# Second self-attention: VectorE's side work moved to between a round's third and fourth maximum, one round later

## The chip, the cores and the metric

The kernel runs on one core of a Trainium2 chip. The metric is the time of one execution on the device in microseconds (us). Below, PE is the matrix engine, DVE the vector engine, ACT the scalar engine, POOL the general-purpose engine, and SP the engine that issues most DMAs; SPq is its queue.

## The reference

Two decoder layers, each of self-attention, cross-attention and a feed-forward block, with a layer norm behind each of the six. The input is 2 x 1024 tokens of 256 numbers. The change lies in the fourth of the six, the self-attention of the second layer, with 16 heads of 16 numbers on 2 batches:

```python
def _layernorm(x, axis=-1, eps=1e-05):
    m = jnp.mean(x, axis=axis, keepdims=True)
    v = jnp.var(x, axis=axis, keepdims=True)
    return (x - m) / jnp.sqrt(v + eps)

def _L1_attn_ref(x, W_qkv, b_qkv, W_proj, b_proj):   # 16 heads of 16, x is (2, 1024, 256)
    B, N, C = x.shape
    qkv = (x @ W_qkv + b_qkv).reshape(B, N, 3, NUM_HEADS, HEAD_DIM)
    q, k, v = jnp.transpose(qkv, (2, 0, 3, 1, 4))
    scores = jnp.einsum('bhqd,bhkd->bhqk', q, k) * SCALE
    attn = jax.nn.softmax(scores, axis=-1)
    out = jnp.einsum('bhqk,bhkd->bhqd', attn, v)
    return jnp.transpose(out, (0, 2, 1, 3)).reshape(B, N, C) @ W_proj + b_proj

x = _layernorm(x + _L0_attn_ref(...), axis=-1)
x = _layernorm(x + _L0_xattn_ref(...), axis=-1)
x = _layernorm(x + _L0_ffn_ref(...), axis=-1)
x = _layernorm(x + _L1_attn_ref(x, L1_attn_W_qkv, L1_attn_b_qkv, L1_attn_W_proj, L1_attn_b_proj), axis=-1)
x = _layernorm(x + _L1_xattn_ref(...), axis=-1)
x = _layernorm(x + _L1_ffn_ref(...), axis=-1)
```

## The kernel before

The program is written engine by engine, with semaphores by hand; nothing reorders it. The second self-attention is in `pe_l1a`, `dve_l1a`, `act_l1a`, `pool_l1a` and `sp_l1a`. It goes over 32 heads (16 per batch) in **rounds** `u` = 0 to 136 (`N_R`); four rounds are one head.

The softmax needs each query's maximum before the exponentials. So the scores are made twice. A first pass makes them with the queries on the partitions, for the maxima alone; a second, some rounds later, makes them with the keys on the partitions, the maximum already taken off through an extra row of the queries' tile. In a round stand:

- **N0 to N3**: four matmuls of the first pass (`natural`, 128x512 each), into banks 0 and 1 in turn. DVE takes the maximum of each: **m0 to m3** (line 1507). N2 waits for m0 and N3 for m1, since they write the same banks; N0 and N1 wait for m2 and m3 of the round before.
- **S**: four matmuls of the second pass (`scores`), for the head of eight rounds ago; ACT makes the exponentials from them (line 1420).
- **W**: the exponentials times the values (`weigh`, 16 matmul records per round), into bank 6.

PE's order in a round is N0, S, N1, N2, W, N3, and then **side work**, which the list `side[u]` sets and which every engine reads. All of it on PE goes through bank 7:

- `rows` (`u` a multiple of 4): PE turns a head's maxima from a column to a row (line 1334), ACT copies the row's leading part (line 1434), DVE takes the rest (line 1536, `s_ml`), and SP writes both into the queries' tile by two DMAs (line 1644).
- `proj` (`u` mod 16 in 1, 3, 5, 7): a quarter of the projection of queries and keys for four heads, six matmuls of 128x512 on PE; ACT takes the leading part out, DVE the rest (`low`, line 1479), which this document calls the **eviction**.
- `values`, `project`, `norm`, `turned`: the values of the second batch (rounds 69 to 72), the output projection of the first batch (rounds 89 to 95), its layer norm in small steps (25 steps for four tiles, from a list `slow`, of which `pump(slow, 4)` takes four in a round), and its transposition (rounds 105 to 111; DVE's part is line 1491). The same list `slow` holds, from round 6 on, the scales of later weights (lines 1457 to 1465, twelve groups of four steps).
- `inverse`: DVE's reciprocals of the softmax's denominators (line 1525), 128x128 each, eight for a group of eight heads. They wait for the DMAs of the group's last head (line 1655), which SP issues, eight for a head in turn into `Zs` and `Zd`, in the round in which that head's sums are ready, behind the `rows` DMAs of the same round. POOL multiplies with them (line 1596).

Where DVE's part of the side work stands, before: the evictions and `turned` go into a list `late` and are done between m0 and m1 of the **next** round; everything else is done right behind m3 of the same round, and then come four steps from `slow`. Every fourth round, m3 is followed by one small reduction (line 1513) that closes a head's maxima.

Of the kernel before, what the change touches and what calls it, by code (L numbers as in the profile page):

```python
# [43 lines left out]
def pump(steps, n):  # L44

    for _ in range(n):
        while steps:
            try:
                next(steps[0])
                break  # L50
            except StopIteration:
                steps.pop(0)
# [21 lines left out]
def program(nc, A, out):  # L74
    ctx = ExitStack()
    with ctx:
        s = {n: ctx.enter_context(nc.semaphore(n)) for n in SEMAPHORES}
# [1139 lines left out]
        N_K = 8 * NH  # L1217
# [6 lines left out]

        side = [[] for _ in range(N_R)]
        for u in range(N_R):
            if u % 4 == 0 and 0 <= (u - 4) // 4 < NH:
                side[u].append(("rows", (u - 4) // 4))
            if 69 <= u < 73:
                side[u].append(("values", 2 * (u - 69)))  # L1230
            if u in (89, 91, 93, 95):
                side[u].append(("project", u - 89))
                if u % 4 == 3:
                    side[u].append(("norm", u - 91))
            if u in (105, 107, 109, 111):
                side[u].append(("turned", (u - 105) // 2))
            if 42 <= u < 128 and u % 32 in (10, 11, 12, 13, 14, 15, 16, 18):
                side[u].append(("inverse", (u - 42) // 32, 128 * (10, 11, 12, 13, 14, 15, 16, 18).index(u % 32), 128))
            if u % 16 in (1, 3, 5, 7) and u // 16 + 1 < 8:
                side[u].append(("proj", u // 16 + 1, (u % 16) // 2))  # L1240
        rest = []
# [232 lines left out]
        def dve_l1a(e, own):  # L1474
            def low(g, u, bk):
                qk, cs, cc = u // 2, slice((u % 2) * 512, (u % 2) * 512 + 512), (C_LQ, C_LK)[u // 2] + g % 4
                hi, lo = TQK[g % 2][qk]
                e.wait_ge(s["s_hi"], 4 * g + u + 1)
                return e.scalar_tensor_tensor(lo[:, cs], PS[:, bk, :], cols[:, cc:cc + 1], hi[:, cs].bitcast(F32),
                                              ALU.add, ALU.subtract)  # L1480

            def values(kt, n, bk):
                shape = dict(a=n, h=16)
                return e.tensor_tensor(V1[:, kt:kt + n, :, 0:16],
                                       PS[:, bk, 0:256 * n].rearrange("p (a h n) -> p a h n", **shape),
                                       rows[:, 2, :].rearrange("p (h n) -> p h n", h=16).unsqueeze(1).to_broadcast([128, n, 16, 16]),
                                       ALU.add)

            def turned(i, bk):
                e.wait_ge(s["t_xh"], 16 + i + 1)  # L1490
                e.tensor_tensor(xl[:, :, i * 256:i * 256 + 256], PS[:, bk, :].rearrange("p (k n) -> p k n", k=2),
                                xh[:, :, i * 256:i * 256 + 256].bitcast(F32), ALU.subtract).then_inc(s["t_xl"], 1)

            for u in range(4):
                low(0, u, u % 2).then_inc(s["s_i"], 1)
            e.wait_ge(s["s_z1"], 1)
            for kt in range(8):
                e.wait_ge(s["s_ip"], 5 + kt)
                values(kt, 1, kt % 2).then_inc(s["s_i"], 1)
            slow, late = [], []  # L1500

            def natural(x, half):
                z, (n, i) = 2 * x + half, divmod(x, 8)
                e.wait_ge(s["s_n"], z + 1)
                if i == 0 and half == 0 and n >= 2:
                    e.wait_ge(s["s_red"], n - 1)
                e.tensor_reduce(nm2[:, n % 2, i, half:half + 1], PS[:, half, :], AX.X, ALU.max,  # L1507
                                negate=True).then_inc(s["s_nr"], 1)
                if z % 16 == 15:
                    e.wait_ge(s["s_nr"], z + 1)  # L1510
                    if n >= 2:
                        e.wait_ge(s["s_p7"], i7["rows", n - 2])
                    e.tensor_reduce(s_nm[:, n % 2, :], nm2[:, n % 2, :, :], AX.X, ALU.min).then_inc(s["s_red"], 1)

            def piece(what):
                if what[0] == "norm":
                    tiles = range(what[1], what[1] + 4)
                    slow.append(norm_steps(e, own, tiles, {j: (s["s_b7"], n_b7["project", j - j % 2]) for j in tiles}))
                elif what[0] in ("proj", "turned"):
                    late.append(what)  # L1520
                elif what[0] == "inverse":
                    _, g, c0, n = what
                    for q in range(2):
                        e.wait_ge(s[f"s_zd{q}"], 128 * (4 * g + 4))
                    e.reciprocal(Zd[:, g % 2, c0:c0 + n], Zd[:, g % 2, c0:c0 + n]).then_inc(s["s_b7"], 1)  # L1525
                elif what[0] == "divide":
                    c0 = what[1]
                    z = Zs[1][:, 1, c0:c0 + 256]
                    e.wait_ge(s["s_b7"], n_b7["inverse", 3, c0, 256])
                    e.tensor_tensor(z, z, Zd[:, 1, c0:c0 + 256], ALU.mult).then_inc(s["s_b7"], 1)  # L1530
                else:
                    e.wait_ge(s["s_p7"], i7[what])
                    if what[0] == "rows":
                        h = what[1]
                        e.wait_ge(s["s_mhd"], h + 1)
                        t = e.tensor_tensor(s_ml[:, h % 2, :], PS[0:8, 7, 0:128], s_mh[:, h % 2, :].bitcast(F32), ALU.subtract)
                    elif what[0] == "values":
                        t = values(what[1], 2, 7)
                    else:
                        jj, bk = what[1], bank7[what]  # L1540
                        e.wait_ge(s["s_xb"], jj + 2)
                        t = e.tensor_tensor(X[:, jj:jj + 2, :], PS[:, bk, :].rearrange("p (a n) -> p a n", a=2),
                                            X[:, jj:jj + 2, :], ALU.add)
                    t.then_inc(s["s_b7"], 1)

            for u in range(N_R):
                x = 2 * u
                if u == 6:
                    slow.append(round_steps(e, own, range(12)))
                if x < N_K:  # L1550
                    natural(x, 0)
                for what in late:
                    if what[0] == "turned":
                        turned(what[1], 7)
                    else:
                        low(what[1], what[2], 7).then_inc(s["s_b7"], 1)
                late = []
                if x < N_K:
                    natural(x, 1)
                    natural(x + 1, 0)  # L1560
                    natural(x + 1, 1)
                for what in side[u]:
                    piece(what)
                pump(slow, 4)
            pump(slow, 99)
            for what in rest:
                piece(what)
                pump(slow, 99)
            for i in range(4, 8):
                turned(i, 2 + i % 2)  # L1570

        def pool_l1a(e):
# [4 lines left out]
            for u in range(N_K // 2):  # L1577
# [3 lines left out]
                if u % 16 == 0 and u // 16 + 1 < 8:  # L1581
                    g = u // 16 + 1
# [5 lines left out]
                    e.tensor_copy(s_wh[:, :], s_wr[:, :]).then_inc(s["s_w"], 1)  # L1588
                    e.wait_ge(s["s_w"], 2 * g + 3)
                    e.tensor_tensor(s_wl[:, :], s_wr[:, :], s_wh[:, :].bitcast(F32), ALU.subtract).then_inc(s["s_w"], 1)  # L1590
                if u >= 52 and u % 32 == 20:
                    g = (u - 52) // 32
                    for half in range(2):
                        z = Zs[g // 2][:, g % 2, half * 512:half * 512 + 512]
                        e.wait_ge(s["s_b7"], n_b7["inverse", g, half * 512 + 384, 128])
                        e.tensor_tensor(z, z, Zd[:, g % 2, half * 512:half * 512 + 512], ALU.mult).then_inc(s["s_zm"], 1)
# [559 lines left out]
        @block.vector  # L2156
        def _(e):
            own = Count(s["dve"])
            dve_l0(e, own)
            dve_rest(e, own)  # L2160
            dve_l1a(e, own)
            dve_l1x(e, own)
            dve_l1f(e, own)

        @block.gpsimd
        def _(e):
            pool_l0(e)
            pool_rest(e)
            pool_l1a(e)
            pool_l1x(e)  # L2170
            pool_l1f(e)
# [78 lines left out]
```

## Time and profile before

| | us |
|---|---|
| three runs, median | 2741.18 |
| lowest, highest | 2738.6, 2742.21 |
| the profiled execution, its own time | 2740.36 |
| its span, first to last instruction | 2738.5 |

| engine | busy us | share of the span |
|---|---|---|
| PE (matmul) | 2453.6 | 90% |
| PEld (weight load, beside PE) | 1710.8 | 62% |
| DVE | 1682.8 | 61% |
| ACT | 1248.4 | 46% |
| POOL | 886.4 | 32% |

The times are of separate executions; the rows below are all of the profiled one, counted from the first instruction of its span. The second self-attention takes the stretch from some 1888 to 2480 us. A row of the timeline gives the start, how long a run of equal instructions took, the engine, the line, the operation and its tiles, the number of instructions, and in brackets how long the engine had been idle and who ended that. In the rows the matmuls N0 to N3 read `PS<-s_K,s_Q`, S reads `PS<-s_Q,s_K`, and W reads `PS<-s_P,s_V`.

### The profile page before, as it was taken

What the parts mean: (1) busy time and instruction counts of PE and PEld (TensorE: products, weight loads), DVE (VectorE), ACT (ScalarE), POOL (GpSimd) and SP (SyncE); (2) the same over time, 40 slices, a digit from 0 to 9 for tenths busy, and PEclk for the clock granted to TensorE, in tenths of its full rate; (3) what the DMA queues carried; (4) which work ended last, traced back from release to release, by engine and by line L of the source; (5) the groups of instructions that cost most, each with busy time, mean ns of one, the idle gap of its engine ahead of it and who ended that gap; (6) DMA issues with size and microseconds to landing.
All of it is one profiled execution on the core that took longest, in us unless ns stands there. A gap on an engine that the chain in (4) does not pass through costs nothing.

```text
span 2738.5 us, 35199 instructions
## 1 busy us (share of the span) xinstructions
PE 2453.6 (90%) x13520; PEld 1710.8 (62%) x13520; DVE 1682.8 (61%) x3009; ACT 1248.4 (46%) x1967; POOL 886.4 (32%) x462
## 2 busy tenths in 40 slices
PE   8999998999999799899999999997898988866763
PEld 7555545744554579788889888995555555534521
DVE  5566655386665335876443444356777778756967
ACT  4555554345555144344444444442565555542442
POOL 4767774366777350102220123001400000004423
PEclk9999999999999999999999999998999999987875
DMA  2000001000000030001010010003243333301000
GB/s 75 13 16 20 12 12 43 12 12 24 12 12 8 22 110 1 31 1 32 31 31 1 31 39 9 1 1 87 57 90 74 76 74 69 72 9 30 1 1 31
DMA packets 57431, 88.08 MB, mean 32 GB/s; under 512 B 13992, under 2 KB 37808, under 8 KB 57264
## 3 DMA queue, kind: packets, MB, share of 16 engines
q1 hardware_dynamic: 57120, 85.77, 12.2%
q8 instruction: 107, 1.75, 0.3%
q14 instruction: 60, 0.49, 0.1%
q10 hardware_dynamic: 144, 0.07, 0.0%
HBM read 37.16 MB, written 2.10 MB: 14 GB/s over the span
## 4 chain that ended last, share of the span: by engine, by line
PE 72%; DVE 18%; issue 3%; ACT 3%; POOL 2%; DMA 1%; SPq 1%; ACTq 0%; DVEq 0%; POOLq 0%
PE PS L85 71%; DVE s_nm L1507 3%; DVE m_gl L1096 2%; DVE PS L575 2%; DVE a_QS L553 1%; ACT a_P L518 1%; DVE a_nm L567 1%; DVE X L270 1%; DVE s_Zd L1525 1%; DVE st_s L231 1%; POOL a_sum L675 1%; DVE x_E L1914 1%; POOL f_H L2119 1%; DVE x_rd L1898 1%; ACT a_QS L472 1%
## 5 line engine op out<-in xcount | busy, mean ns | idle before, releaser
L675 POOL TENSOR_TENSOR a_sum<-a_sum,a_P 128x1024 f32<-128x1024 f32 x192 | 456.2, 2376 | 128.6 <-ACT a_P L518 118.2
L1096 DVE TENSOR_TENSOR m_gl<-m_g,m_gh 128x512 fp32r<-128x512 f32 x288 | 258.1, 902 | 386.4 <-ACT m_g L935 386.4
L518 ACT ACTIVATE a_P<-PS 128x512 f32<-128x512 f32 x512 | 290.1, 596 | 354.7 <-PE PS L85 349.9
L932 ACT ACTIVATE m_gh<-PS,cols 128x512 fp32r<-128x512 f32 x288 | 198.3, 689 | 470.1 <-PE PS L85 470.1
L1507 DVE TENSOR_REDUCE s_nm<-PS 128x1 f32<-128x512 f32 x512 | 336.5, 683 | 106.1 <-PE PS L85 103.2
L567 DVE TENSOR_REDUCE a_nm<-PS 128x1 f32<-128x1024 f32 x256 | 300.4, 1216 | 128.0 <-PE PS L85 128.0
L85 PE MATMUL PS<-m_w2h,m_gh 128*128 128x256 f32 x1152 | 325.2, 282 | 18.9 <-DVE m_gl L1096 18.7
L85 PE MATMUL PS<-m_w2l,m_gh 128*128 128x256 f32 x1152 | 323.8, 281 | 0.0
L85 PE MATMUL PS<-m_w2h,m_gl 128*128 128x256 f32 x1152 | 323.6, 281 | 0.0
L1420 ACT ACTIVATE s_P<-PS 128x1024 f32<-128x1024 f32 x256 | 248.1, 1021 | 127.7 <-PE PS L85 127.3
L85 PE MATMUL PS<-s_K,s_Q 128*128 128x512 f32 x512 | 218.1, 464 | 46.7 <-DVE s_nm L1507 43.7
L85 PE MATMUL PS<-a_P,a_V 128*64 128x512 f32 x1024 | 250.8, 612 | 0.0
L85 PEld LDWEIGHTS PS<-m_w2h,m_gh 128*128 128x128 f32 x1152 | 218.2, 189 | 35.2 <-DVE m_gl L1096 23.6
L85 PE MATMUL PS<-xh,m_w1h 128*128 128x512 f32 x576 | 231.0, 401 | 0.0
L85 PE MATMUL PS<-xh,m_w1l 128*128 128x512 f32 x576 | 227.1, 394 | 0.0
L85 PE MATMUL PS<-a_QS,a_KH 128*128 128x512 f32 x512 | 220.1, 430 | 7.7 <-ACT a_P L518 7.7
L85 PE MATMUL PS<-xl,m_w1h 128*128 128x512 f32 x576 | 225.9, 392 | 0.0
L85 PEld LDWEIGHTS PS<-m_w2h,m_gl 128*128 128x128 f32 x1152 | 219.1, 190 | 10.6
L85 PEld LDWEIGHTS PS<-m_w2l,m_gh 128*128 128x128 f32 x1152 | 218.6, 190 | 0.0
L1151 POOL CAST m_w1h<-m_raw 128x2048 fp32r<-128x2048 f32 x9 | 20.5, 2283 | 603.8 <-PE PS L85 594.1
L85 PE MATMUL PS<-a_QM,a_KL 128*128 128x512 f32 x512 | 202.1, 395 | 0.0
L935 ACT ACTIVATE m_g<-PS,cols 128x512 f32<-128x512 f32 x288 | 196.1, 681 | 0.0
(296 smaller groups left out, 4192.6 us busy)
## 6 DMA issues: line engine op xcount, KB each, us to landing
m_raw<-in_m_w SPq DMA_DIRECT2D x16, 1024.0 KB, 5.1
s_Q<-s_T SPq DMA_DIRECT2D x128, 128.0 KB, 2.4
s_K<-s_T SPq DMA_DIRECT2D x128, 128.0 KB, 2.4
a_KH<-a_KH SPq DMA_DIRECT2D x64, 128.0 KB, 2.4
a_wr<-in_w_qk SPq DMA_DIRECT2D x16, 256.0 KB, 2.8
X<-in_x SPq DMA_DIRECT2D x4, 512.0 KB, 6.1
a_P<-in_w_v SPq DMA_DIRECT2D x8, 256.0 KB, 5.8
a_P<-in_w_o SPq DMA_DIRECT2D x2, 1024.0 KB, 6.0
```

The lines of the kernel that those rows point to most:

```text
L85: return e.matmul(o, l, r, start=start, stop=stop, skip_group_check=shared)
L231: e.bn_stats(st_s[:, j, :], X[:, j, :]).then_inc(own.sem, 1)
L270: e.tensor_scalar(X[:, j, :], X[:, j, :], st_a[:, j, 0:1], st_r[:, 0, j:j + 1], ALU.subtract, ALU.mult).then_inc(s["normed"], 1)
L518: e.activation(a_P[:, g % N_P, half * 512:half * 512 + 512], PS[:, 2 + half, :], ACT.Exp).then_inc(s["a_exp"], 1)
L567: e.tensor_reduce(a_nm[:, n % 2, 8 * a + i:8 * a + i + 1], PS[:, bk:bk + 2, :], AX.XY, ALU.max, negate=True).then_inc(s["a_max"], 1)
L575: e.reciprocal(r, r).then_inc(own.sem, 1)
L675: e.tensor_tensor(o[:, :], a_P[:, (g - 1) % N_P, :] if k == 1 else o[:, :], a_P[:, g % N_P, :], ALU.add).then_inc(s["a_add"], 1)
L932: e.activation(m_gh[r][:, :], PS[:, 4 + n % 3, :], func, bias=cols[:, bcol:bcol + 1]).then_inc(s["m_gh"], 1)
L935: e.activation(m_g0[r][:, :], PS[:, 4 + n % 3, :], func, bias=cols[:, bcol:bcol + 1]).then_inc(s["m_g0"], 1)
L1096: e.tensor_tensor(m_gl[r][:, :], m_g0[r][:, :], m_gh[r][:, :].bitcast(F32), ALU.subtract).then_inc(s["m_gl"], 1)
L1420: e.activation(s_P[w % 4][:, :].rearrange("p (a n) -> p a n", a=2), PS[:, bk:bk + 2, :], ACT.Exp, scale=0.25).then_inc(s["s_exp"], 1)
L1507: e.tensor_reduce(nm2[:, n % 2, i, half:half + 1], PS[:, half, :], AX.X, ALU.max, negate=True).then_inc(s["s_nr"], 1)
```

## The change

DVE's order in a round becomes m0, m1, m2, then all side work that the round **before** left (`late`), then four steps from `slow`, then m3. `values` alone stays behind m3 of its own round. The reciprocals are listed one round later (and the last three at other distances), so that the first group's run in rounds 44 to 49, 51 and 53 instead of behind m3 of rounds 42 to 48 and 50, and the next two groups' 32 and 64 rounds later; POOL's two multiplications with them move from round 52 to round 54. In round 72, PE makes the values before it turns the maxima.

```diff
         for u in range(N_R):
+            if 69 <= u < 73:
+                side[u].append(("values", 2 * (u - 69)))
             if u % 4 == 0 and 0 <= (u - 4) // 4 < NH:
                 side[u].append(("rows", (u - 4) // 4))
-            if 69 <= u < 73:
-                side[u].append(("values", 2 * (u - 69)))
...
-            if 42 <= u < 128 and u % 32 in (10, 11, 12, 13, 14, 15, 16, 18):
-                side[u].append(("inverse", (u - 42) // 32, 128 * (10, 11, 12, 13, 14, 15, 16, 18).index(u % 32), 128))
+            if 43 <= u < 128 and u % 32 in (11, 12, 13, 14, 15, 16, 18, 20):
+                side[u].append(("inverse", (u - 42) // 32, 128 * (11, 12, 13, 14, 15, 16, 18, 20).index(u % 32), 128))
...
-                elif what[0] in ("proj", "turned"):
-                    late.append(what)
+                elif what[0] == "turned":
+                    turned(what[1], 7)
+                elif what[0] == "proj":
+                    low(what[1], what[2], 7).then_inc(s["s_b7"], 1)
...
                 if x < N_K:
                     natural(x, 0)
-                for what in late:
-                    if what[0] == "turned":
-                        turned(what[1], 7)
-                    else:
-                        low(what[1], what[2], 7).then_inc(s["s_b7"], 1)
-                late = []
-                if x < N_K:
                     natural(x, 1)
                     natural(x + 1, 0)
+                for what in late:
+                    piece(what)
+                late = [what for what in side[u] if what[0] != "values"]
+                pump(slow, 4)
+                if x < N_K:
                     natural(x + 1, 1)
                 for what in side[u]:
-                    piece(what)
-                pump(slow, 4)
+                    if what[0] == "values":
+                        piece(what)
+            for what in late:
+                piece(what)
             pump(slow, 99)
...
-                if u >= 52 and u % 32 == 20:
-                    g = (u - 52) // 32
+                if u >= 54 and u % 32 == 22:
+                    g = (u - 54) // 32
```

What this does to the order of instructions is seen on DVE. First the place of an eviction (`s_T`) that is followed by a row's rest (`s_ml`), in rounds 36 and 37; maxima are the rows with 128x1, the small reduction that closes a head is the row with 128x8. Before:

```order
L1513 TENSOR_REDUCE s_nm<-s_nm 128x8
L1507 TENSOR_REDUCE s_nm<-PS 128x1
L1479 SCALAR_TENSOR_TENSOR s_T<-PS,cols,s_T 128x512
L1507 TENSOR_REDUCE s_nm<-PS 128x1 x3
L1536 TENSOR_TENSOR s_ml<-PS,s_mh 8x128
L1507 TENSOR_REDUCE s_nm<-PS 128x1 x5
```

And changed:

```order
L1513 TENSOR_REDUCE s_nm<-s_nm 128x8
L1507 TENSOR_REDUCE s_nm<-PS 128x1 x3
L1479 SCALAR_TENSOR_TENSOR s_T<-PS,cols,s_T 128x512
L1507 TENSOR_REDUCE s_nm<-PS 128x1 x4
L1538 TENSOR_TENSOR s_ml<-PS,s_mh 8x128
L1507 TENSOR_REDUCE s_nm<-PS 128x1 x4
```

The eviction went from behind the first maximum of its round to behind the third, and the row's rest from behind the fourth maximum of that round to behind the third of the next.

The second place is DVE at the first reciprocals of a group (`s_Zd`, from round 42 on). Before:

```order
L1536 TENSOR_TENSOR s_ml<-PS,s_mh 8x128
L1507 TENSOR_REDUCE s_nm<-PS 128x1 x8
L1525 RECIPROCAL s_Zd<-s_Zd 128x128
L1507 TENSOR_REDUCE s_nm<-PS 128x1 x4
L1513 TENSOR_REDUCE s_nm<-s_nm 128x8
L1525 RECIPROCAL s_Zd<-s_Zd 128x128
L1507 TENSOR_REDUCE s_nm<-PS 128x1 x4
```

And changed:

```order
L1538 TENSOR_TENSOR s_ml<-PS,s_mh 8x128
L1507 TENSOR_REDUCE s_nm<-PS 128x1 x9
L1513 TENSOR_REDUCE s_nm<-s_nm 128x8
L1507 TENSOR_REDUCE s_nm<-PS 128x1 x3
L1527 RECIPROCAL s_Zd<-s_Zd 128x128
L1507 TENSOR_REDUCE s_nm<-PS 128x1 x4
```

The first reciprocal stood behind the fourth maximum of round 42 and stands now behind the third of round 44, seven maxima later; the row's rest ahead of it is itself later by three.

## Rows read from the trace of the kernel before

**Rows 1.** The chain that ended last, 1888 to 2430 us, shares by line:

```profile
by line: PE PS L85 68.9%; DVE s_nm L1507 14.2%; issue 4.4%; DVE s_Zd L1525 3.1%; SPq L1655 1.8%; DVE s_ml L1536 1.5%; DMA s_Zd<-s_zt 0.7%; DVE f_ws L1457 0.6%; SPq L1644 0.5%; DMA s_K<-s_T 0.5%; DVE X L1542 0.4%; DVE s_T L1479 0.4%; ACT s_P
```

**Rows 2.** Two stretches: us, busy PE, PEld, DVE, ACT, POOL; granted clock; DMA:

```profile
1960.00:2024.00 64.00, 62.63 (x444) 36.99 (x443) 50.01 (x88) 38.77 (x48) 6.33 (x6) 1.00 0.37 83
...
2062.00:2064.00 2.00, 2.00 (x17) 0.60 (x16) 0.70 (x2) 0.00 (x0) 0.00 (x0) 0.50 0.99 215
```

**Rows 3.** Timeline, a round without side work:

```profile
1995.18 0.73 PE L85 MATMUL PS<-s_K,s_Q 128*128 128x512 f32 x2
1995.72 2.67 DVE L1507 TENSOR_REDUCE s_nm<-PS 128x1 f32<-128x512 f32 x4 [0.69 <-PE PS L85]
...
1997.06 0.19 PEld L85 LDWEIGHTS PS<-s_K,s_Q 128*128 128x128 f32 x1 [0.41 <-DVE s_nm L1507]
1997.49 1.07 PE L85 MATMUL PS<-s_P,s_V 128*32 128x256 f32 x16
1999.03 2.67 DVE L1507 TENSOR_REDUCE s_nm<-PS 128x1 f32<-128x512 f32 x4 [0.64 <-PE PS L85]
```

**Rows 4.** Timeline, rounds with a reciprocal: N2, then m3 and the next m3:

```profile
2071.56 0.50 PE L85 MATMUL PS<-s_K,s_Q 128*128 128x512 f32 x1 [0.86 <-DVE s_nm L1507]
...
2073.53 0.69 DVE L1507 TENSOR_REDUCE s_nm<-PS 128x1 f32<-128x512 f32 x1 [0.74 <-PE PS L85]
...
2077.64 0.69 DVE L1507 TENSOR_REDUCE s_nm<-PS 128x1 f32<-128x512 f32 x1 [0.73 <-PE PS L85]
```

**Rows 5.** Timeline, DVE: m3 before and behind a round with a group of weight scales:

```profile
1931.49 0.69 DVE L1507 TENSOR_REDUCE s_nm<-PS 128x1 f32<-128x512 f32 x1 [0.74 <-PE PS L85]
...
1935.50 0.69 DVE L1507 TENSOR_REDUCE s_nm<-PS 128x1 f32<-128x512 f32 x1 [0.74 <-PE PS L85]
```

**Rows 6.** Timeline, a round with an eviction (PE and DVE), up to its m3:

```profile
1988.99 0.39 PE L85 MATMUL PS<-s_K,s_Q 128*128 128x512 f32 x1
...
1989.42 0.69 DVE L1507 TENSOR_REDUCE s_nm<-PS 128x1 f32<-128x512 f32 x1 [0.72 <-PE PS L85]
...
1990.02 0.74 DVE L1479 SCALAR_TENSOR_TENSOR s_T<-PS,cols,s_T 128x512 fp32r<-128x512 f32 x1
...
1990.13 0.61 PE L85 MATMUL PS<-s_K,s_Q 128*128 128x512 f32 x2
...
1990.68 1.28 DVE L1507 TENSOR_REDUCE s_nm<-PS 128x1 f32<-128x512 f32 x2
...
1992.02 0.28 PE L1334 MATMUL PS<-ident,s_nm 128*8 128x128 f32 x1
...
1992.22 0.69 DVE L1507 TENSOR_REDUCE s_nm<-PS 128x1 f32<-128x512 f32 x1 [0.26 <-PE PS L85]
```

**Rows 7.** Timeline, the first reciprocal of a group and the DMAs it waits for:

```profile
2051.71 0.68 SPq L1644 DMA_DIRECT2D s_Q<-s_mh  x1
...
2057.61 0.69 DVE L1507 TENSOR_REDUCE s_nm<-PS 128x1 f32<-128x512 f32 x1 [0.63 <-PE PS L85]
...
2058.03 0.59 SPq L1655 DMA_DIRECT2D s_Zd<-s_zt  x1
...
2059.92 0.95 DVE L1525 RECIPROCAL s_Zd<-s_Zd 128x128 f32<-128x128 f32 x1 [1.61 <-DMA s_Zd<-s_zt]
...
2061.47 0.80 PE L85 MATMUL PS<-s_K,s_Q 128*128 128x512 f32 x1 [2.51 <-DVE s_nm L1507]
...
2062.20 1.94 PE L85 MATMUL PS<-s_P,s_V 128*32 128x256 f32 x16
...
2064.90 0.69 DVE L1507 TENSOR_REDUCE s_nm<-PS 128x1 f32<-128x512 f32 x1 [1.90 <-PE PS L85]
```

**Rows 8.** Timeline, DVE: m3 ahead of the third group's first reciprocal, and the two next:

```profile
2330.82 0.69 DVE L1507 TENSOR_REDUCE s_nm<-PS 128x1 f32<-128x512 f32 x1 [0.33 <-PE PS L85]
...
2338.32 0.69 DVE L1507 TENSOR_REDUCE s_nm<-PS 128x1 f32<-128x512 f32 x1 [1.90 <-PE PS L85]
...
2343.23 0.69 DVE L1507 TENSOR_REDUCE s_nm<-PS 128x1 f32<-128x512 f32 x1 [0.36 <-PE PS L85]
```

## The prediction, made blind

> **What bounds it now.** I went from the page to the chain of waits, then to the busy time by stretch, and from there to the timeline of single rounds. The chain through the second self-attention is two engines taking turns: PE 68.9% on the matmul line, DVE 14.2% on the maxima, 3.1% on the reciprocals and small shares of the row's rest and the weight scales [rows 1]. By busy time PE looks full in the middle of it, 62.63 of 64 us [rows 2]. The timeline says more [rows 3]. In a round without side work, N3 starts at 1995.18 and m3 0.54 later; m3 and m0 to m2 of the next round follow each other without a gap, four in 2.67, so 0.67 each. N2's weight load is released at 1997.06, the moment m0 ends (1995.72 + 2 x 0.67), W starts 0.43 later, and 1.00 behind W the next N3. That is a loop: 0.54 + 0.67 + 0.67 + 0.43 + 1.00 = 3.31 us, and m3 to m3 is 3.31 (1995.72 to 1999.03). What stands on DVE between m3 and m0 lengthens this loop by all that it takes. But ahead of m3 DVE is idle for 0.64, since m2 ends while PE is in W: that gap is where the change puts the work.
>
> **Side work in the gap.** A piece of length d costs d now, and max(0, d - 0.64) in the gap.
>
> 1. Reciprocals. With one behind m3 the round is 4.11 (2073.53 to 2077.64) [rows 4], so d = 4.11 - 3.31 = 0.80; in the gap 0.16 is left. 3 groups of 8: 24 x 0.64 = 15.4 saved. Where a row's rest shares the round the saving is the same 0.64.
> 2. Weight scales. 4.01 from m3 to m3 [rows 5], d = 0.70, of which 0.06 is left. Twelve groups; the three ahead of the first W, and what then overlaps an eviction, I count for nothing: 9 x 0.64 = 5.8.
> 3. Rows' rests. 1992.22 to 1995.72 is 3.50 [rows 3, 6], d = 0.19, wholly covered. Of 32, only seven stand in a round whose gap is otherwise empty and that follows no eviction: 1.3.
> 4. The layer norm's steps, four to a round like the scales and of like length. Six rounds without an eviction, at 0.64, one of them shared with a row: 3.6.
> 5. The wait for the denominators' DMAs. In two of three groups the first reciprocal holds DVE 1.61 us [rows 7] and more: these rounds take 7.29 (2057.61 to 2064.90) and 7.50 [rows 7, 8] where 4.11 is usual, and the one behind the second 4.91 (2338.32 to 2343.23) where 4.3 is (4.11 and the row's 0.19). 3.2 + 3.4 + 0.6 = 7.2. Part of it is the clock: behind 2.51 us of idle PE, N2 takes 0.80 and W 1.94, against 0.50 and 1.07, at a granted 0.50 [rows 2 to 4, 7]. Does the wait come back? SP issues in order. The row's two DMAs wait for its rest, which is now behind m2 of the next round, some 2.0 us (three maxima) later; the last denominator DMA stands 6.32 behind the first of them (2051.71, 2058.03), so it goes out near 2060.0 and, landing 1.9 later as now (2058.03 to 2059.92), is there at 2061.9. The reciprocal has moved by seven maxima: m3 of its old round at 2057.61, one plain round of 3.31, then m3 itself and m0 to m2, 2.67, makes 2063.6. It comes 1.7 behind the data. I take the whole 7.2.
>
> Saved: 15.4 + 5.8 + 1.3 + 3.6 + 7.2 = 33.3.
>
> **What the move costs.**
>
> 6. Evictions. They now stand between m0 and m1, which costs nothing: m1 must wait for N1 anyway. m0 starts 0.43 behind N0's start (1988.99, 1989.42), so m1 could start 0.43 behind N1's 1990.13, at 1990.56, and m2 end 1.28 later, at 1991.84 [rows 6]. The eviction (0.74, of which 0.14 overlaps with its neighbours as m0's start and m1's show: 0.60) would then end at 1992.44, while m3's data are there at 1992.22. With what a start costs (0.02 to 0.04), 0.26 per eviction; it stays in the loop because the next m0 is behind m3. 28 run in the rounds; the first three have no W behind them and DVE works there without a gap either way: 25 x 0.26 = 6.5.
> 7. Bank 7. In 14 rounds PE turns a row straight behind an eviction. It does so at 1992.02 now [rows 6] and must wait until 1992.5, with N0, S and N1 behind it. N2 follows N0 by 1.36 (1988.99 to 1990.35, below) and N0 the turn by some 0.1: 1994.0. m0, behind an m3 that starts at 1992.48, ends at 1993.8, and N2's weights take up to 0.19 from there [rows 3]. So 0 to 0.2 shows; 0.13 taken: 14 x 0.13 = 1.8.
> 8. Collisions. In four rounds an eviction and norm steps, which are both hidden today (one between m0 and m1, the other behind a PE busy with the projection), meet in one gap: the steps' 0.70 finds no room there; I take 0.5 each, between 0 and 0.70, 2.0. DVE's four `turned` pieces move like evictions, 4 x 0.25 = 1.0, and three of them meet a reciprocal whose saving of item 1 is then gone, 3 x 0.64 = 1.9. The four output projections, 0.1 each: 0.4. These are estimates from the rows of the single pieces.
>
> Costs: 6.5 + 1.8 + 2.0 + 2.9 + 0.4 = 13.6. Edits that I put at nothing: POOL's multiplications two rounds later (their results are wanted at round 89 or past the end) and the swap of values and rows in round 72 (bank 7 makes one wait for the other either way).
>
> **Sum.** 33.3 - 13.6 = 19.7 less. The profiled execution took 2740.36 (span 2738.5); 2720.7. It lies 0.8 under the median of the three runs, 2741.18, so against that: 2721.
>
> **Bounds.** The gap shows as 0.64 in a plain round, 0.74 where there is side work [rows 3, 4] and 0.26 in an eviction round [rows 6]. Its pieces have their round to themselves, so 0.64 is the nearest; at 0.74 some 38 whole uses give 3.8 more, and at 0.26 they give 14 less, which I hold for far. An eviction costs between 0 (6.5 better) and its whole 0.74 (25 x 0.48 = 12 worse). Of item 5, at worst the DMA wait proper comes back, 2 x 1.7 = 3.4. Together 8 better to 12 or 13 worse.
>
> **Rivals.**
>
> *Evictions cost their whole length.* If m1 and m2 run late after a projection (or PE, held at bank 7, makes them late), no gap is left in those rounds and all 0.74 lies in the loop: 12 worse, 2733. For it: only 0.26 is idle there [rows 6]. Against it: m2 ends 0.4 ahead of m3's data by the same rows.
>
> *PE is the bound, and nothing moves.* If the matmuls need the 3.31 themselves, DVE's order is free: 2741. For it: PE busy 98% [rows 2]. Against it: from N0 to N2 is 1.36 in the eviction round (1988.99; the pair that starts at 1990.13 takes 0.61 and its second 0.39 of that, so N2 starts at 1990.35) and 1.54 in the plain one (N0 at 1995.18 + 0.73 - 0.39 = 1995.52, N2 at 1997.06), so PE waits 0.18 while it counts as busy; and with a reciprocal it stands 0.86 before N2, released by a maximum [rows 3, 4, 6]. The Trainium skill, "Perfetto Trace Analysis", section "Identifying the Most-Contended Engine", says to take the engine with the highest occupancy and optimise that first, which here is PE, so that by it this reordering of DVE saves nothing. The same section calls matmul occupancy a poor measure; the 0.18 of waiting inside busy time agrees with that.
>
> *The clock falls, slower.* If PE, waiting at bank 7 or at N1 behind a late eviction, were idle long enough for its clock to fall to the lower level, as it did to 1.2 GHz in the DMA wait, each such round would pay what that one did beyond the wait: 7.29 less 3.31, 0.80 and 1.65 (m3's end to the reciprocal's start, 2058.27 to 2059.92) = 1.53. 25 x 1.53 = 38, so 2741 - 20 + 38 = 2759. It decides between 0.86 us of idle, where N2 still takes 0.50, and 2.51, where it takes 0.80 [rows 4, 7]; item 7 makes 0.5.
>
> **How the numbers follow.** Forecast 0.80, costly evictions 0.13, PE the bound 0.04, clock 0.03. Range 2713 to 2734: the forecast with its bounds, and the first rival. 0.2% is 5.5 us, about what a measurement of this kernel can tell: above 2735.7 is no change. The forecast and nearly all of the first rival lie below: faster 0.91, same 0.06, slower 0.03.
>
> **What would show it.** Reciprocal rounds at 3.45 to 3.6 instead of 4.11 to 4.3; scale rounds at 3.35; row rounds that follow no eviction at 3.31; eviction rounds at 4.7 instead of 4.42, counted from m3 to m3; no idle time of DVE before a reciprocal; plain rounds unchanged at 3.31. It is wrong if plain rounds change, if SP's gathers come late, if a reciprocal still waits for its DMA, or if eviction rounds exceed 5.

## The result, and the profile after

| | before | after |
|---|---|---|
| median of the runs, us (4 and 4) | 2739.89 | 2714.89 |
| lowest and highest | 2734.14, 2742.21 | 2713.13, 2717.37 |
| the profiled execution, its own time (span) | 2740.36 (2738.5) | 2717.37 (2715.5) |

The ratio is 0.9912, with a 95% interval of 0.9894 to 0.9931: faster by 0.9%, 25.0 us, where 19.7 were forecast. From m3 of round 0 to m3 of round 127 the changed kernel takes 493.32 us instead of 519.73, 26.41 less in the profiled pair, so the whole gain lies in these rounds. The profiled executions differ by only 23.0: the one of after reaches its first maximum 2.7 later, in stages that the change does not touch, and takes 0.8 more behind the last m3.

The chain that ended last, shares by line, changed kernel, 1888 to 2410 us:

```profile
by line: PE PS L85 64.9%; DVE s_nm L1507 21.8%; DVE s_T L1479 3.6%; issue 2.2%; DVE s_Zd L1527 1.5%; PE PS L1334 0.9%; SPq L1627 0.6%; DMA s_K<-s_T 0.5%; DVE X L1544 0.5%; DVE xl L1491 0.5%; DVE st_s L231 0.4%; SPq L1657 0.4%; DVE s_V L1484
```

Against [rows 1], the reciprocals' share is halved (3.1% to 1.5%). The weight scales and the row's rest (0.6% and 1.5%) no longer stand among the shares shown, nor does the DMA into `s_Zd`. The matmul line fell from 68.9% to 64.9%, and the maxima rose from 14.2% to 21.8%. The evictions came in, with 3.6% instead of 0.4%, and the turn through bank 7 with 0.9%: the price that the prediction expected.

Busy time and clock of 64 us in the middle, in the order of [rows 2]:

```profile
1957.00:2021.00 64.00, 62.67 (x453) 36.83 (x446) 50.15 (x89) 39.10 (x49) 6.34 (x6) 1.00 0.41 92
```

PE counts as busy for 62.67 of 64 us where it was 62.63 [rows 2], at the same granted clock. This view alone shows neither the gain that was to be had nor the one that was made.

Timeline of DVE, changed kernel, the rounds of the first reciprocals:

```profile
2059.38 0.69 DVE L1507 TENSOR_REDUCE s_nm<-PS 128x1 f32<-128x512 f32 x1 [0.63 <-PE PS L85]
...
2062.08 0.94 DVE L1527 RECIPROCAL s_Zd<-s_Zd 128x128 f32<-128x128 f32 x1
2062.94 1.25 DVE L1507 TENSOR_REDUCE s_nm<-PS 128x1 f32<-128x512 f32 x2
...
2065.81 0.93 DVE L1527 RECIPROCAL s_Zd<-s_Zd 128x128 f32<-128x128 f32 x1
2066.67 2.50 DVE L1507 TENSOR_REDUCE s_nm<-PS 128x1 f32<-128x512 f32 x4
2069.08 0.94 DVE L1527 RECIPROCAL s_Zd<-s_Zd 128x128 f32<-128x128 f32 x1
2069.94 2.62 DVE L1507 TENSOR_REDUCE s_nm<-PS 128x1 f32<-128x512 f32 x4
2072.48 0.94 DVE L1527 RECIPROCAL s_Zd<-s_Zd 128x128 f32<-128x128 f32 x1
2073.34 0.63 DVE L1507 TENSOR_REDUCE s_nm<-PS 128x1 f32<-128x512 f32 x1
```

The maximum behind a reciprocal is an m3. From m3 to m3 the rounds take 3.56 (2059.38 to 2062.94), 3.73 with a row's rest in it, 3.27 (2066.67 to 2069.94) and 3.40, against 4.11 [rows 4]. DVE has no idle time left ahead of m3. The first reciprocal waits for nothing; the last DMA for it was issued here:

```profile
2058.43 0.59 SPq L1657 DMA_DIRECT2D s_Zd<-s_zt  x1
```

With the 1.9 that such a DMA took [rows 7] its data are there at 2060.3, 1.75 ahead of the reciprocal at 2062.08. The prediction said 1.7.

Timeline of DVE, changed kernel, two rounds with weight scales:

```profile
1934.15 2.61 DVE L1507 TENSOR_REDUCE s_nm<-PS 128x1 f32<-128x512 f32 x4
1936.68 0.41 DVE L1457 TENSOR_REDUCE f_ws<-f_w 128x1 f32<-128x256 f32 x1
1937.13 0.15 DVE L1461 TENSOR_SCALAR f_ws<-f_ws 128x1 f32<-128x1 f32 x1
1937.31 0.16 DVE L1465 RECIPROCAL f_ws<-f_ws 128x1 f32<-128x1 f32 x1
1937.44 2.68 DVE L1507 TENSOR_REDUCE s_nm<-PS 128x1 f32<-128x512 f32 x4
```

m3 to m3 is 3.29 (1934.15 to 1937.44), where such a round took 4.01 [rows 5].

Timeline of PE and DVE, changed kernel, the eviction round that answers to [rows 6]:

```profile
1985.51 0.69 DVE L1507 TENSOR_REDUCE s_nm<-PS 128x1 f32<-128x512 f32 x1 [0.73 <-PE PS L85]
...
1988.25 1.29 DVE L1507 TENSOR_REDUCE s_nm<-PS 128x1 f32<-128x512 f32 x2 [0.46 <-PE PS L85]
...
1989.45 0.74 DVE L1479 SCALAR_TENSOR_TENSOR s_T<-PS,cols,s_T 128x512 fp32r<-128x512 f32 x1
1990.11 1.38 DVE L1507 TENSOR_REDUCE s_nm<-PS 128x1 f32<-128x512 f32 x2
...
1990.25 0.27 PE L1334 MATMUL PS<-ident,s_nm 128*8 128x128 f32 x1 [0.38 <-DVE s_T L1479]
```

The eviction now stands between m2 (behind m1 at 1988.25) and m3 (1990.11). The round is 4.60 (1985.51 to 1990.11), 0.18 longer than the 4.42 of before. PE waits 0.38 at bank 7 for the eviction. Plain rounds are 3.31 as before.

The stage by the prediction's items, its counts shared out over the rounds, from the starts of m3 in both traces (us; each round's difference, summed):

| rounds | predicted | measured |
|---|---|---|
| weight scales, with what is counted for evictions and bank 7 in these rounds (1 to 17) | -5.3 | -5.46 |
| rows' rests alone (seven rounds) | -1.3 | -1.35 |
| norm steps (93 to 103, odd) | -3.6 | -4.33 |
| the reciprocals' rounds with the DMA wait and the evictions and `turned` among them (43 to 57, 75 to 89, 107 to 117) | -17.1 | -21.27 |
| eviction and norm in one gap (98 to 104, even) | +3.3 | +3.15 |
| output projections (90 to 96, even) | +0.4 | -0.32 |
| other evictions and bank 7 | +3.9 | +3.17 |
| sum | -19.7 | -26.41 |

### The profile page after: what moved, and what is told of

Read it like the earlier page. It is cut to its first block, busy times and chain, and to the rows that moved or that the text cites. A ratio compares the mean times of both kernels' runs of the same rounds, so it can differ in the third digit from the quotient of the medians.

```text
span 2715.5 us, 35197 instructions
## 1 busy us (share of the span) xinstructions
PE 2450.4 (90%) x13518; PEld 1709.8 (63%) x13520; DVE 1686.8 (62%) x3009; ACT 1250.1 (46%) x1967; POOL 886.2 (33%) x462
## 3 DMA queue, kind: packets, MB, share of 16 engines
q8 instruction: 107, 1.75, 0.3%
## 4 chain that ended last, share of the span: by engine, by line
PE 71%; DVE 20%; issue 3%; ACT 3%; POOL 2%; DMA 1%; SPq 0%; ACTq 0%; DVEq 0%; POOLq 0%
PE PS L85 70%; DVE s_nm L1507 4%; DVE m_gl L1096 2%; DVE PS L575 2%; DVE a_QS L553 1%; ACT a_P L518 1%; DVE a_nm L567 1%; DVE X L270 1%; DVE s_T L1479 1%; DVE x_E L1916 1%; DVE x_rd L1900 1%; DVE st_s L231 1%; POOL f_H L2121 1%; POOL a_sum L675 1%; ACT a_QS L472 0%
```

## The experiments

The theory is the prediction's: the loop m3, m0, N2, W, N3, m3 is the bound, side work outside it is free up to the gap's length, and reciprocals listed later don't wait for their DMAs. The rivals are that only idle time seen ahead of m3 is free, that PE is the bound, and that the whole gain is the DMA wait. Every ratio is to the kernel before, of runs on the same chip.

### Only the reciprocals later, still behind m3

From the kernel before; POOL's multiplications move with them:

```diff
-            if 42 <= u < 128 and u % 32 in (10, 11, 12, 13, 14, 15, 16, 18):
+            if 44 <= u < 128 and u % 32 in (12, 13, 14, 15, 16, 17, 18, 20):
```

> The kernel before, with one edit: the reciprocals (and the multiplications behind them) are listed two rounds later, still behind the fourth maximum, and nothing else moves. Loop theory (the change gains by its place: side work behind m0 and ahead of m3 is covered by the loop's slack, and behind m3 it is not): only the wait for the denominators' DMAs goes, some 7 us less than before (ratio 0.997), and rounds with a reciprocal stay at 4.1 to 4.3 us from m3 to m3. Rival (PE is the bound, the whole gain of the change is the DMA wait and the clock that fell with it): all of the change's 25 us, ratio 0.991.

Median 2733.19 (12 runs) against 2739.39 (17); ratio 0.9977 [0.9962, 0.9992]. DVE's timeline:

```profile
2072.67 0.69 DVE L1507 TENSOR_REDUCE s_nm<-PS 128x1 f32<-128x512 f32 x1 [0.74 <-PE PS L85]
2073.28 0.94 DVE L1525 RECIPROCAL s_Zd<-s_Zd 128x128 f32<-128x128 f32 x1
...
2076.79 0.69 DVE L1507 TENSOR_REDUCE s_nm<-PS 128x1 f32<-128x512 f32 x1 [0.74 <-PE PS L85]
```

No reciprocal waits for a DMA any more and the stage is 8.0 shorter (511.77), near the 7.2 of item 5. The rounds still take 4.12 (2072.67 to 2076.79), with 0.74 idle ahead of m3 that nothing uses. The later table alone buys the DMA wait, with the low clock that came with it, and nothing else; the rest is the place in the round.

### The changed order with the reciprocals one round earlier

From the changed kernel, the table of before:

```diff
-            if 43 <= u < 128 and u % 32 in (11, 12, 13, 14, 15, 16, 18, 20):
+            if 42 <= u < 128 and u % 32 in (10, 11, 12, 13, 14, 15, 16, 18):
```

> The changed kernel with the reciprocals listed as in the kernel before, so that they run one round earlier than in the changed kernel, at the same place between m2 and m3. By its trace the first reciprocal of a group comes 1.7 us behind its data; one round is 3.3 us. Loop theory with item 5 of the prediction: the first reciprocal of the first and third group waits for its DMA again, some 1.6 us, and the clock may fall with it: 3 to 7 us more than the changed kernel, ratio to before 0.992 to 0.994. Rival (the DMA wait had gone because of the place, not of the later round): as the changed kernel, ratio 0.991, no idle time before a reciprocal.

Median 2720.61 (6 runs); ratio 0.9935 [0.9920, 0.9950], stage 500.46. DVE's timeline at the first reciprocal:

```profile
2048.77 2.67 DVE L1507 TENSOR_REDUCE s_nm<-PS 128x1 f32<-128x512 f32 x4 [0.64 <-PE PS L85]
2053.01 0.95 DVE L1527 RECIPROCAL s_Zd<-s_Zd 128x128 f32<-128x128 f32 x1 [1.56 <-DMA s_Zd<-s_zt]
2053.88 0.63 DVE L1507 TENSOR_REDUCE s_nm<-PS 128x1 f32<-128x512 f32 x1
```

The wait is back, 1.56 against 1.61 [rows 7], and the round (2048.77 to 2053.88) takes 5.11 where it is 3.31 in the changed kernel. With the rows' rests one round later, SP's DMAs are later too: the last one goes out 2.34 behind the m3 shown first (at 2051.11), where it was 0.42 before (2058.03 behind 2057.61 [rows 7]). The expectation named the first and the third group; the second waits too, 2.27, and the third 1.96. Against the changed kernel the stage is 7.1 longer. So the delay of the table was needed for this order.

### How much fits into the gap

From the changed kernel: reciprocals of ones, whose result nobody reads, in plain rounds between m2 and m3, two rounds of each width up to 128 columns, one of 160; and one behind m3 of round 126:

```diff
+            PAD = {26: 32, 27: 32, 30: 64, 31: 64, 58: 96, 59: 96, 62: 112, 63: 112, 118: 128, 119: 128, 122: 160}
...
                 pump(slow, 4)
+                if u in PAD:
+                    padded(PAD[u])
                 if x < N_K:
                     natural(x + 1, 1)
+                if u == 126:
+                    padded(64)
```

> The changed kernel plus 11 useless reciprocals on a tile of their own, each in a round without any side work, between m2 and m3, in widths of 32 (rounds 26, 27), 64 (30, 31), 96 (58, 59), 112 (62, 63), 128 (118, 119) and 160 (122), and one of 64 behind m3 of round 126. The output is the reference's. From the reciprocals of 128 and 256 (0.94 and 1.75 us, 0.14 overlapped) these are pieces of length 0.19, 0.40, 0.60, 0.70, 0.80 and 1.00. Loop theory: rounds without side work are 3.31; 26 to 63 stay so, 118 and 119 become 3.4, 122 becomes 3.6, and the one behind m3 costs its whole 0.40 (round 127 at 3.7). If the gap were the 0.64 that the prediction read from the idle time, 62 and 63 would be 3.37 and 118, 119 3.47. Rival (PE is the bound in such rounds): all at 3.31 up to 1.0, the one behind m3 too.

One run (2715.5 us); the rounds are read within its trace. DVE's timeline at 112 columns, then behind m3 of round 126 (maxima are line 1514 here):

```profile
2124.37 2.68 DVE L1514 TENSOR_REDUCE s_nm<-PS 128x1 f32<-128x512 f32 x4 [0.33 <-PE PS L85]
2126.97 0.84 DVE L1507 RECIPROCAL s_pad<-ones 128x112 f32<-128x112 f32 x1
2127.73 2.62 DVE L1514 TENSOR_REDUCE s_nm<-PS 128x1 f32<-128x512 f32 x4
2130.27 0.84 DVE L1507 RECIPROCAL s_pad<-ones 128x112 f32<-128x112 f32 x1
2131.03 0.65 DVE L1514 TENSOR_REDUCE s_nm<-PS 128x1 f32<-128x512 f32 x1
...
2384.55 0.69 DVE L1514 TENSOR_REDUCE s_nm<-PS 128x1 f32<-128x512 f32 x1 [0.62 <-PE PS L85]
2385.15 0.54 DVE L1507 RECIPROCAL s_pad<-ones 128x64 f32<-128x64 f32 x1
...
2388.26 0.69 DVE L1514 TENSOR_REDUCE s_nm<-PS 128x1 f32<-128x512 f32 x1 [0.74 <-PE PS L85]
```

Records of 0.34, 0.54 and 0.74 leave the round at 3.30 to 3.31. At 0.84 the first round is 3.36 (2124.37 to 2127.73) and the second 3.30 (to 2131.03); at 0.94 they are 3.28 and 3.39, where the changed kernel without them has 3.22 and 3.31; at 1.145 the round is 3.66, and the next one gives 0.05 back (3.26). Behind m3, a record of 0.54 makes the round 3.71 (2384.55 to 2388.26): 0.40 dearer, all of it but the 0.14 that overlaps. So a piece is free between m2 and m3 up to a record of some 0.84, that is a length of 0.70, and costs its whole length behind m3. PE is not the bound: a wait that DVE puts into the loop shows at once.

### Evictions back between m0 and m1, the rest in the gap

From the changed kernel:

```diff
                     natural(x, 0)
+                for what in late:
+                    if what[0] in ("proj", "turned"):
+                        piece(what)
...
                 for what in late:
-                    piece(what)
+                    if what[0] not in ("proj", "turned"):
+                        piece(what)
```

> The changed kernel, with the evictions and the turned pieces back between m0 and m1, where the kernel before has them; all other side work stays between m2 and m3. Loop theory: eviction rounds go from 4.6 to 4.8 us back to 4.42, and the four rounds in which an eviction meets norm steps from 5.05 to 5.4 back to some 4.5; 10 us less than the changed kernel, 35 less than before (ratio 0.987). Rival (the place does not matter, only that work is a round later, or PE is the bound): as the changed kernel, ratio 0.991.

Median 2702.91 (4 runs); ratio 0.9868 [0.9852, 0.9883], stage 482.62: faster than both kernels. PE and DVE at the eviction round answering to the one above:

```profile
1981.58 0.69 DVE L1507 TENSOR_REDUCE s_nm<-PS 128x1 f32<-128x512 f32 x1 [0.56 <-PE PS L85]
...
1983.81 0.74 DVE L1479 SCALAR_TENSOR_TENSOR s_T<-PS,cols,s_T 128x512 fp32r<-128x512 f32 x1
1984.46 1.28 DVE L1507 TENSOR_REDUCE s_nm<-PS 128x1 f32<-128x512 f32 x2
...
1985.81 0.27 PE L1334 MATMUL PS<-ident,s_nm 128*8 128x128 f32 x1
1986.01 1.29 DVE L1507 TENSOR_REDUCE s_nm<-PS 128x1 f32<-128x512 f32 x2 [0.27 <-PE PS L85]
```

The round is 4.43 (1981.58 to 1986.01), and PE turns the row without waiting. The four collisions fall from 5.42, 5.31, 5.25 and 5.05 to 4.85, 4.77, 4.72 and 4.48, the three rounds in which `turned` meets a reciprocal from 4.50, 4.26 and 4.44 to 4.07, 3.79 and 4.01. These are the costs of items 6 to 8, most of them undone; the four collisions still stand above the 4.62 and three times 4.42 of before.

### Evictions alone between m2 and m3, all else as before

From the kernel before, the loop over `late` moved behind m1 and m2 (behind `natural(x + 1, 0)`).

> The kernel before with one edit: the evictions and the turned pieces stand between m2 and m3 of their round instead of between m0 and m1; all else as before. Loop theory: eviction rounds go from 4.42 to 4.6 to 4.8, without the collisions with norm steps; some 6 to 7 us more than before, ratio 1.0025. Rival (an eviction is hidden by PE's projection wherever it stands): ratio 1.000.

Median 2742.83 (11 runs) against 2738.89 (15); ratio 1.0018 [1.0007, 1.0028], stage 526.83. Eviction rounds take 4.59 to 4.64, and rows' rounds behind one 3.72 instead of 3.50. This is the one part of the change that costs, and it costs without any of the others: by the stage 7.1, where items 6 and 7 and the 1.0 for `turned` say 9.3.

### All side work between m0 and m1

From the changed kernel, `late` and `pump(slow, 4)` moved from behind m2 to behind m0 (ahead of `natural(x, 1)`).

> The changed kernel, with all side work that stands between m2 and m3 moved to between m0 and m1. Loop theory: what is released by m0 is N2 and so W, and everything behind m0 and ahead of m3 has the same slack, so reciprocal and scale rounds stay at 3.3 to 3.5, and the evictions fall into the wait for N1: 9 to 10 us less than the changed kernel, ratio to before 0.988. Rival (only the idle time that the profile shows ahead of m3 is free, and whatever delays m1 delays N3 and m3): reciprocal rounds at 4.0 or more, the time back at that of before or above it, ratio 1.0.

Median 2703.62 (5 runs); ratio 0.9871 [0.9850, 0.9891], stage 483.07. DVE's timeline at the reciprocals:

```profile
2057.73 0.93 DVE L1527 RECIPROCAL s_Zd<-s_Zd 128x128 f32<-128x128 f32 x1
2058.59 2.49 DVE L1507 TENSOR_REDUCE s_nm<-PS 128x1 f32<-128x512 f32 x4
2061.00 0.94 DVE L1527 RECIPROCAL s_Zd<-s_Zd 128x128 f32<-128x128 f32 x1
2061.86 2.65 DVE L1507 TENSOR_REDUCE s_nm<-PS 128x1 f32<-128x512 f32 x4
```

The maximum behind a reciprocal is here an m1, and m1 to m1 is 3.27 (2058.59 to 2061.86). From m3 to m3, rounds 44 to 49 take 3.31 to 3.52, closing reductions and rows' rests included. In a plain round DVE is idle for only 0.10 between m0 and m1 (m0 ends at 1996.32 + 0.68 and m1 starts at 1997.10 in the round of [rows 3], which leave so short a gap unmarked), and yet a reciprocal is all but free there. The rival that only idle time seen ahead of m3 is free falls: what is free is what the loop does not contain.

### All side work between m1 and m2

From the changed kernel, the same two lines moved to behind m1 (ahead of `natural(x + 1, 0)`).

> The changed kernel with all side work between m1 and m2 instead of between m2 and m3. Loop theory: rounds with a reciprocal or a scale alone stay at 3.3 to 3.5, since m1 and m2 are both behind m0; the evictions stand behind m1, which waits for N1, so they cost about as much as behind m2. As the changed kernel or up to 4 us more: ratio to before 0.991 to 0.993, and 11 to 15 us more than with all between m0 and m1. Rival (work must stand ahead of m3 to be free): reciprocal rounds at 4 or more, ratio 1.0.

Median 2727.99 (5 runs); ratio 0.9956 [0.9944, 0.9969]: a miss, as neither number came. In the first two groups, behind the group's first (3.52), rounds with a reciprocal alone take 3.83 to 3.85, with a closing reduction 3.90 to 3.92, with a row's rest 3.93 to 4.06; scales alone 3.73 to 3.74. The stage is 506.30. PE and DVE at a reciprocal:

```profile
2071.82 1.90 DVE L1507 TENSOR_REDUCE s_nm<-PS 128x1 f32<-128x512 f32 x3
2072.49 0.50 PE L85 MATMUL PS<-s_K,s_Q 128*128 128x512 f32 x1 [0.71 <-DVE s_nm L1507]
2072.82 1.09 PE L85 MATMUL PS<-s_Q,s_K 128*128 128x512 f32 x4
2073.75 0.63 PE L85 MATMUL PS<-s_K,s_Q 128*128 128x512 f32 x2
2074.19 0.69 DVE L1507 TENSOR_REDUCE s_nm<-PS 128x1 f32<-128x512 f32 x1 [0.47 <-PE PS L85]
...
2074.79 0.94 DVE L1527 RECIPROCAL s_Zd<-s_Zd 128x128 f32<-128x128 f32 x1
...
2075.65 1.91 DVE L1507 TENSOR_REDUCE s_nm<-PS 128x1 f32<-128x512 f32 x3
```

There is a second loop that I had not written down. N0 (2072.49) waits 0.71 for m2 (2071.82), S and N1 follow on PE, m1 (2074.19) waits 0.47 for N1, and m2 (2075.65) comes behind the reciprocal. That is 0.67 + 1.70 + 1.46 = 3.83, the round as measured. With m1's own 0.67 in the place of the 1.46 it would be 3.04, so this loop has 0.27 to spare against 3.31, and a length of 0.80 shows as 0.53. For the scales' 0.70 it gives 3.74, again as measured. With a reciprocal and a row's rest (0.80 + 0.19) it gives 4.03, for 3.93 to 4.06. Rounds 55 and 116, which hold nothing between m1 and m2 and follow a round that does, show the loop bare: m2 to m2 is 3.04 and 3.05 in them. That this is the cause in every one of these rounds was read from this one timeline and from these periods, not from a further run.

### Evictions, `turned` and the output projection between m0 and m1

As in "Evictions back between m0 and m1, the rest in the gap", with `project` added to the tuple.

> The changed kernel with evictions, turned pieces and the output projections between m0 and m1, the rest between m2 and m3. Loop theory: as with the evictions alone between m0 and m1, and rounds 92, 94 and 96 go from 6.2, 5.6, 5.6 to some 5.8, 5.1, 5.1: 1 to 2 us less than that one, 37 to 38 less than before, ratio 0.986. Rival (the place of the projections does not matter): the same as that one, 0.9868.

Median 2702.03 (4 runs); ratio 0.9862 [0.9847, 0.9877], stage 481.47. Rounds 92, 94 and 96 fall to 5.67, 5.04 and 5.02, from 6.23, 5.61 and 5.57 with only evictions and `turned` moved. Its time can't be told from the two other versions that keep evictions between m0 and m1; all three beat the changed kernel, by intervals that end below its 0.9894.

## Why the prediction was right, and where its sizes were off

**The loop (what bounds it).** Right. Plain rounds stay at 3.31, pieces behind m3 cost their length and pieces outside the loop do not, up to the room there. It is not the only loop: a second, of 3.04, decides between m1 and m2 and is not in the prediction, which did not need it. The measured median, 2714.89, lies near the fast end of the range, and by the table the misses do not cancel: the large ones all lie on the side of more gain than forecast.

**Items 1 to 4, the saved lengths.** The mechanism was right; the step that was mis-sized is "a piece of length d costs max(0, d - 0.64) in the gap". The room is some 0.70 in a plain round, as the added reciprocals show, and the leftover does not add up from round to round as I summed it. Part of the reason stands in DVE's rows. In a plain round m3 and the three maxima behind it take 2.67 [rows 3], not "without a gap", as the prediction reads it, but with the 0.10 in which m1 waits for N1. In the round that starts behind a reciprocal at 2066.67, m1 waits for nothing, and the four take 2.50. DVE catches up. I had 3.47 for such a round (3.31 + 0.16); the one from 2066.67 to 2069.94 is 3.27. Over rounds 44 to 49 a reciprocal saved 0.72 in the mean (4.29 in six rounds), between 0.56 (round 49, 4.30 to 3.74) and 0.84 (round 46, 4.12 to 3.28), where I had 0.64.

**Item 5, the DMA wait.** Right, with the clock's part in it: rounds 43 and 107 fall from 7.28 and 7.50 to 3.31 and 3.30, which is 0.80 for the reciprocal and 3.2 and 3.4 for the wait. The reciprocals left later alone gave 8.0.

**Items 6 and 7, evictions and bank 7.** Right in kind: eviction rounds that follow no reciprocal are mostly 0.17 to 0.26 longer, against 0.26 (of which the 0.02 to 0.04 for a start stands in no row), and rounds 22 and 38, two rounds behind a hold at bank 7, 0.37 and 0.41. But the eviction rounds 50, 54, 82 and 86 got 0.22 to 0.24 shorter (4.44 to 4.20 in round 50), where I had added 0.26 each: these rounds follow one with a reciprocal and a row's rest, and the leftover lateness seems to come back there, as it did in the round behind the widest added reciprocal. Rounds 52 and 84, which follow a reciprocal alone (round 51 has 3.34, so next to nothing is left over), got 0.12 and 0.18 longer. No run was made to part the two. A hold at bank 7 cost 0.19 where 0.13 was taken: the rows' rounds 21, 25 and 37 stay at 3.48 to 3.50 in the changed kernel and take 3.31 to 3.32 with the evictions back between m0 and m1. Of the 4.2 by which the reciprocals' rounds beat the forecast, some 2 lie in these four.

**Item 8, collisions.** 3.15 measured for 3.3, an estimate that was near. The output projections cost nothing; they saved 0.32.

**The rivals.** *Evictions cost their whole length* would have put an eviction round at 5.16 (4.42 + 0.74); the one above is 4.60. *PE is the bound* falls with PE's 62.67 of 64 us and 26 us less of stage. The rule of the Trainium skill ("Perfetto Trace Analysis", "Identifying the Most-Contended Engine") to optimise the engine with the highest occupancy first did not lead here; its remark that matmul busy time is not a good measure of how close one is to roofline fits these two numbers. *The clock falls*: the granted clock is 1.00 in the changed kernel from 1928 to 2389 us. The waits at bank 7, from the list of waits of the changed kernel, 1888 to 2405 us (us in total, times, longest):

```profile
PE PS L1334 <- DVE s_T L1479: 5.7, 13, 0.8
```

None exceeds the 0.86 of idle that left N2 at 0.50 [rows 4]. The prediction looks for what decides between 0.86 and 2.51 of idle; the length of one idle stretch is not all of it. With the reciprocals one round early, the clock fell to 0.50 behind the first group's wait, for which PE stood idle 1.36 before N2, and stayed at 1.00 behind the second's, with 2.08.

**What was not seen.** The prediction asked whether evictions fit into the gap, not whether they should be in it. Kept between m0 and m1 they cost next to nothing, and the change would have been worth 1.3%.

## What to carry to other kernels

When two engines take turns, write down each closed loop of waits through one round, with its length, before moving work: a piece is free where it lies in no loop, or in one with that much to spare, and idle time shown in the trace is only a hint of that (0.64 shown ahead of m3 held 0.70; in a plain round DVE idles 0.10 ahead of m1 and not at all ahead of m2, and 0.80 went all but free into the one place, 0.27 by the second loop's length into the other). Side work of different lengths may want different places. And a step moved later delays the transfers that it starts: move what waits for them by as much.

## What the runs showed that was not expected

DVE's records overlap. In a plain round (from 1995.72) the maxima of 128x512 start 0.61, 0.78 and 0.61 apart, and the 0.78 holds the 0.10 of waiting for N1; in the round from 2066.67, where DVE waits for nothing, 0.55, 0.67 and 0.61, though their records last 0.62 to 0.69. A reciprocal of 128x128 has a record of 0.94, but the maximum behind it starts 0.86 after its start, and it adds 0.80 to a round.
